# Cross-attention on one core: the value product stands ahead of the transposes in each sub-step of TensorE

## The reference

```
qh = _split_heads(q @ wq.T + bq, h)
kh = _split_heads(k @ wk.T + bk, h)
vh = _split_heads(v @ wv.T + bv, h)
scores = jnp.einsum('ntd,nsd->nts', qh, kh) / jnp.sqrt(jnp.asarray(depth, qh.dtype))
scores = scores + km * PAD
attn = jax.nn.softmax(scores, axis=-1)
ctx = jnp.einsum('nts,nsd->ntd', attn, vh)
out = _merge_heads(ctx, h) + q
mu = jnp.mean(out, axis=-1, keepdims=True)
var = jnp.var(out, axis=-1, keepdims=True)
out = (out - mu) / jnp.sqrt(var + LN_EPS) * gamma + beta
```

## Time and profile before

| what | value |
|---|---|
| median of 3 runs | 1205.42 us (1205.4 to 1206.03) |
| the profiled execution, span | 1203.9 us |
| TensorE matmul busy | 1131.0 us (94%) |
| VectorE busy | 989.6 us (82%) |
| GpSimd busy | 885.7 us (74%) |
| ScalarE busy | 671.2 us (56%) |
| granted TensorE clock, mean | 0.991 |
| DMA | 131.89 MB, mean 110 GB/s |

### The profile page before, as it was taken

How to read it: one execution, slowest core, us unless ns; L and a number is a source line. 1 busy time by engine, 2 the same in 40 slices (tenths; PEclk the granted TensorE clock), 3 DMA queues, 4 the chain that set the end, 5 groups by cost and what they waited for, 6 DMA issues and landing times.

```text
span 1203.9 us, 25840 instructions
## 1 busy us (share of the span) xinstructions
PE 1131.0 (94%) x7536; PEld 1037.6 (86%) x7536; DVE 989.6 (82%) x1773; ACT 671.2 (56%) x1131; POOL 885.7 (74%) x711
## 2 busy tenths in 40 slices
PE   8999899999999999999999999999999999999994
PEld 7888788889888888888898888888888988888983
DVE  4221789898888889998988888899989888888887
ACT  5221555666655656556666556665566665565551
POOL 1300436888888888888888888888888888888886
PEclk9999999999999999999999999999999999999996
DMA  7643123333333333333333333233333332332223
GB/s 266 227 143 124 49 81 90 115 103 111 110 82 105 97 91 111 115 115 106 109 113 107 88 98 97 91 112 115 115 106 110 113 107 83 103 99 90 72 79 132
DMA packets 114998, 131.89 MB, mean 110 GB/s; under 512 B 50548, under 2 KB 59764, under 8 KB 114836
## 3 DMA queue, kind: packets, MB, share of 16 engines
q1 hardware_dynamic: 114964, 131.45, 35.0%
HBM read 87.60 MB, written 43.80 MB: 109 GB/s over the span
## 4 chain that ended last, share of the span: by engine, by line
PE 62%; DVE 14%; issue 11%; POOL 1%; ACT 1%; DVEq 1%; POOLq 0%
PE q_ps L614 22%; PE o_ps L656 19%; PE s_ps L631 12%; PE t_ps L642 9%; DVE probs L798 3%; DVE attn L713 2%; DVE q_lo L788 2%; DVE row_max L806 2%; DVE inv_sum L701 1%; DVE x_lo L774 1%; POOL probs L912 1%; DVE bd_lo L782 1%; DVE stats L721 1%; DVE attn L752 0%; PE q_ps L656 0%
## 5 line engine op out<-in xcount | busy, mean ns | idle before, releaser
L912 POOL TENSOR_TENSOR probs<-probs,row_max 128x616 f32<-128x616 f32 x255 | 320.2, 1256 | 188.5 <-DVE row_max L806 186.9
L656 PE MATMUL o_ps<-v_tiles,pt 128*128 128x66 f32 x2520 | 312.5, 271 | 35.1 <-DVE attn L713 35.1
L656 PEld LDWEIGHTS o_ps<-v_tiles,pt 128*128 128x128 f32 x2520 | 302.1, 192 | 42.6 <-issue 25.5
L944 ACT ACTIVATE probs<-probs 128x616 f32<-128x616 f32 x256 | 183.3, 716 | 264.1 <-POOL probs L912 259.8
L614 PE MATMUL q_ps<-x_lo,wq_hi 128*128 128x512 f32 x500 | 217.6, 435 | 12.1 <-DVE q_lo L788 10.1
L798 DVE TENSOR_TENSOR probs<-s_ps,mask_pad 128x616 f32<-128x616 f32 x256 | 202.4, 791 | 28.8 <-PE s_ps L631 28.7
L806 DVE TENSOR_REDUCE row_max<-probs 128x8 f32<-128x616 f32 x256 | 202.6, 791 | 12.1
L614 PE MATMUL q_ps<-x_hi,wq_hi 128*128 128x512 f32 x500 | 197.9, 396 | 0.0
L614 PE MATMUL q_ps<-x_hi,wq_lo 128*128 128x512 f32 x500 | 197.2, 394 | 0.0
L891 POOL TENSOR_TENSOR y<-y,beta_all 128x512 f32<-128x512 f32 x123 | 179.4, 1459 | 9.6
L975 ACT COPY pt<-t_ps 128x512 f32<-128x512 f32 (+1 forms) x320 | 173.8, 584 | 12.7 <-PE t_ps L642 9.7
(11 more groups left out here) (89 smaller groups left out, 1622.4 us busy)
## 6 DMA issues: line engine op xcount, KB each, us to landing
xT_raw<-in_xT SPq DMA_DIRECT2D x32, 1024.0 KB, 5.4
x_rows<-in_x SPq DMA_DIRECT2D x32, 1024.0 KB, 5.5
out<-y SPq DMA_DIRECT2D x128, 256.0 KB, 2.1
k_scratch<-k_out SPq DMA_DIRECT2D x8, 616.0 KB, 4.4
k_raw<-k_scratch SPq DMA_DIRECT2D x32, 154.0 KB, 2.3
v_scratch<-v_out SPq DMA_DIRECT2D x16, 264.0 KB
v_tiles<-v_scratch SPq DMA_DIRECT2D x256, 9.9 KB
ctx_raw<-in_ctxT SPq DMA_DIRECT2D x3, 1232.0 KB, 7.3
```

Source lines behind the costliest of these rows:

```text
L656: mm = pe.matmul(bank_of(b, t)[:, col:col + tile_cols[i]], pt[h][0:w, i, P * t:P * t + P], v_tiles[v_buffer(b, h)][0:w, i, 0:tile_cols[i]] ...
L912: pool.tensor_tensor(v, v, row_max[:, u, :].unsqueeze(2).broadcast_to([P, HH, S]), ALU.subtract).then_inc(shifted, 1)
L944: act.activation(probs[h][:, t, :], probs[h][:, t, :], ACT.Exp).then_inc(exp_done, 1)
```

## The change

In `step` of the tensor block, the product moves ahead of the transposes wherever both stand in a sub-step; the special case of the last step goes away, since every step now has that order. The operations, their waits and their signals are the same.

```diff
                         if real(a):
                             scores(a, h, t, par)
-                        last_turns = is_last(a - 1) and h == 0
-                        if last_turns:
-
+                        if real(a - 1):
                             product(a - 1, h, t)
                         if real(a - 1 + h):
                             for i in TURNS[t]:
                                 turn(a - 1 + h, 1 - h, i)
-                        if real(a - 1) and not last_turns:
-                            product(a - 1, h, t)
 
                 steps(pe, step)
```

## The result

The changed kernel takes 1201.49 us (median of 8 runs, 1200.83 to 1204.08) against 1205.41 us before (8 runs): 3.9 us or 0.33% less between the medians. The ratio estimated from all these runs is 0.9973, 95% interval 0.9963 to 0.9983; the forecast was 1203.2 us. The profiled execution has a span of 1201.5 us where the one of before had 1203.9; it is the one of 1203.28 us, the second longest of the eight. The lines of VectorE, ScalarE and GpSimd have moved up by four: L713 is now L709, L788 is L784, L975 is L971, L912 is L908.

A forecast was written before the change was run, and what follows sets the result against it. TensorE was taken to bound each period's first half, VectorE the second. Waits 0, boundaries -2.7, delayed ScalarE work +0.5, start and end 0 sum to -2.2 us: span 1201.7, time 1203.2 us, range 1199.5 to 1210.5.

The forecast's parts named there:

- the boundaries: TensorE switching between transposes, product and projection in s5 to s7: 0.03 us saved at 90 places, -2.7 us (-4.5 to +2.7).
- start and end: Last step already in the new order, last item's earlier steps paced by VectorE and GpSimd: priced 0.
- rival 1: Transposes, ScalarE's copies and x_hi come late behind the new wait, delaying VectorE: 1210.8 us at 0.3 us per item; chance 0.20.
- The waits only move: TensorE's waits for VectorE in s1 to s4 change place, total lateness stays 1.83 us per item: priced 0.
- Behind the new wait: ScalarE's x_hi and q_hi, delayed in s2 to s3, keep 0.03 and 0.15 us in hand: priced +0.5 us over 27 items.
- Rival 2: TensorE's boundaries cost the same in either order, leaving only the order of waits: 1205.4 us, give or take 1; chance 0.25.
- Rival 3: TensorE's waits for VectorE (35.1 + 10.1 us) really go, needing unseen slack on VectorE: about 1160 us; chance 0.05.

The follow-up runs named there:

- E1: Kernel before, with the value product ahead of the transposes only in an item's second four sub-steps (h=1) and, as before, the last step: 1198.79 us, ratio 0.9941.
- E4: The changed kernel itself, run again beside other variants on their chip, against the kernel before: 1203.51 us, ratio 0.9973.
- E7: Kernel before, with three quarters of the keys' low part on VectorE left out in sub-step s4: 1197.12 us, ratio 0.9919.
- E3: Changed kernel, with h=0 in the old order and the product between the two transpose tiles in s5 and s6, first in s7: 1199.91 us, ratio 0.9950.
- E9: Kernel before, with VectorE's keys' low part moved behind the scaling of the product in s1 to s4: 1179.58 us, ratio 0.9781.
- E6: Changed kernel plus one added copy on ScalarE in s3, its result unused: 1208.96 us, ratio 1.0033.
- E10: Changed kernel, with VectorE's keys' low part moved behind the scaling of the product in s1 to s4: 1213.78 us, ratio 1.0072.

## Why the prediction was right

The time lies 1.7 us below the forecast of 1203.2 and inside the range; faster by over 0.2%, which came, had a chance of 0.32, within 0.2% had 0.48. The mechanism was right, but that the sum came so near is in part luck: -2.7 us for the boundaries should have been -4.7 over all items, 0 for start and end should have been +2.1 (E1 against E4), and 0.5 for rival 1 in the middle items should have been 0.2 at most. The forecast has -2.2 and the items in the profiled executions -2.5, since these errors cancel. By its steps:

- *The waits only move.* Right. P(2) waits anew, Q(4) no longer, P(4) still; lateness 0.68 + 1.11 against the 0.75 + 1.08 worked out, the product's waits 48.5 us against "some 50", those of the projection 1.2 us. VectorE's chain is 17.02 us as before. That the chain is VectorE's own work was wrong (E7): a good part is time behind GpSimd. For this change that made no difference, since both queues ran the same course as before in h=0; for the price of other edits it is decisive.
- *The boundaries.* Right in kind, undersized in the sum. The row that I trusted only in part gave 1.85, and 1.86 was measured against 1.91 before in s5 and s6 (means over 24 items); I took -0.03 for each of 90 places. The sub-steps s5, s6 and s7 shrank by 0.04, 0.065 and 0.06 (medians over 24 items), the stretch from P(4) to P(0) by some 0.17 us. E1 shows it alone: 893.85 - 889.62 = 4.2 us in the 27 middle items, 4.7 with those at either side. That is just past the end of -4.5, not at -2.7.
- *Behind the new wait.* Right in the middle items, to 0.05 us: x_hi 0.08 us in hand (0.03 worked out), q_hi 0.14 (0.15). The step that failed is the one that let "start and end" be nothing. In the items 2 and 30 VectorE comes to q_lo sooner, since x_lo takes 0.69 us or isn't there at all, and the cover is gone. VectorE in item 2 of the kernel before, then in item 2 and in item 30 of the changed kernel:

```profile
198.04 0.68 DVE L774 TENSOR_TENSOR x_lo<-xT_raw,x_hi 128x512 fp32r<-128x512 f32 x1
198.64 0.74 DVE L788 SCALAR_TENSOR_TENSOR q_lo<-q_ps,bq_col,q_hi 128x512 fp32r<-128x512 f32 x1
```

```profile
198.91 0.69 DVE L770 TENSOR_TENSOR x_lo<-xT_raw,x_hi 128x512 fp32r<-128x512 f32 x1
200.10 0.75 DVE L784 SCALAR_TENSOR_TENSOR q_lo<-q_ps,bq_col,q_hi 128x512 fp32r<-128x512 f32 x1 [0.50 <-ACT q_hi L965]
```

```profile
1122.51 0.75 DVE L784 SCALAR_TENSOR_TENSOR q_lo<-q_ps,bq_col,q_hi 128x512 fp32r<-128x512 f32 x1 [0.87 <-ACT q_hi L965]
```

In item 1 q_lo waits 0.48 us where it didn't before, in item 30 0.87 where it was 0.24, in item 31 2.29 where it was 1.50. So rival 1 did come, in four items of 32. It cost 2.1 us there (E4 against E1), and with what the boundaries save in the same items, 1.6 us of the 4.1 were taken back. Working through one item near either end as through the one in the middle could have shown this, and E1 as the better change, before any run.
- *Rival 2* (boundaries alike) is out by E1 and E3, and with it that the eighteen loads take the same time in either order. *Rival 3* (the waits really go) is out for this change. Its premise, slack inside VectorE's chain, was true all the same: E9 has it, 26 us, by an order on VectorE and not on TensorE.

## What to carry to other kernels

A wait that moves is not a wait that goes: work out the lateness of each queue before and after, and ask what the releasing engine itself stands behind. Where VectorE and GpSimd both work on SBUF, read an operation's duration against its size: a 32x77 operation of 1.25 us is a wait without a name, and moving the whole operation off the path gained 26 us in the kernel before, more than any order on TensorE. Check an edit to a pipelined loop on the first and last items too. Two edits that each gain can lose together, here 8 us where they gained 26 and 7 alone, when one shifts which of two engines is first and holds up the other.

## What the runs showed of the hardware

The end of the kernel, some 50 us, differed between executions by up to 3.3 us, and with it the granted clock. Windows of TensorE's tail (us, busy us and count of PE, PEld, DVE, ACT, POOL, then PEclk, DMA share, GB/s), first in E1 and then in E4:

```profile
1169.00:1174.00 5.00, 3.09 (x29) 2.88 (x29) 4.79 (x13) 1.25 (x3) 4.75 (x4) 1.00 0.68 208
1174.00:1179.00 5.00, 4.33 (x40) 4.08 (x38) 1.61 (x6) 4.13 (x7) 2.18 (x4) 1.00 0.42 161
```

```profile
1171.00:1176.00 5.00, 4.47 (x23) 4.10 (x22) 4.79 (x12) 1.17 (x2) 4.75 (x4) 0.51 0.54 163
1176.00:1181.00 5.00, 5.00 (x26) 5.00 (x26) 1.08 (x5) 1.17 (x2) 0.95 (x2) 0.50 0.54 206
```

Just ahead of these windows TensorE idles three times in both, 0.74, 0.67 and 0.67 us in E1 and 0.73, 0.68 and 0.68 in E4. After that it kept 2.4 GHz in E1, and was granted 1.2 GHz for some 10 us in E4: 50.74 us against 47.47 for the last stretch of the table. In the traces of E3 and E6, which also had no 1.2 GHz while TensorE still worked there, that stretch took 47.45 and 47.48 us; in E9, with some 10 us of it, 50.49; in the nine others, with some 3 to 7 us, 48.0 to 49.6. So executions of one kernel differ by the clock of the tail: the E4 runs of 1200.6 to 1201.4 us had a mean granted clock of 0.992, those of 1203.5 to 1204.5 one of 0.988 to 0.990.

E1's distance to E4 in the medians, 4.7 us, holds only 2.1 us that the items account for. Between the two profiled executions the tail gives another 3.3. What decides which clock an execution gets there, the runs don't show. The stretch ahead of item 1 differs too, with Q(0) of item 1 between 149.75 us (E10) and 152.24 us (the changed kernel); why is open.
